# First layer's context attention: key projection of two slabs by seven products, context in two slots

## The reference

```python
def _L0_xattn_ref(query_tokens, key_tokens, key_down, query_down, query_down_bias, value_down, value_up):
    # H, T, A, C = (8, 512, 64, 128)
    def swishmax(x, axis):
        m = jnp.max(x, axis=axis, keepdims=True)
        xe = x * jnp.exp(x - m)
        return xe / (jnp.sum(jnp.abs(xe), axis=axis, keepdims=True) + 1.0)
    k = jnp.einsum('bkt,hta->bhka', key_tokens, key_down)
    q = jnp.einsum('bqt,hta->bhqa', query_tokens, query_down) + query_down_bias[None]
    logits = jnp.einsum('bhka,bhqa->bhkq', k, q)
    attn = swishmax(logits, axis=-2)
    vs = jnp.einsum('bhkq,bkt->bhqt', attn, key_tokens)
    vs = jnp.einsum('bhqc,hct->bhqt', jnp.einsum('bhqt,htc->bhqc', vs, value_down), value_up)
    return vs.sum(axis=1)
...
    x = x + _L0_xattn_ref(_layernorm(x, axis=-1), ctx_1024, L0_xattn_key_down, ...)
```

## Time and profile before

| | us |
|---|---|
| median of 3 runs | 4138.32 (4137.81 to 4142.93) |
| the profiled execution, its own time | 4137.65 |
| its span, first to last instruction | 4135.9 |
| TensorE busy | 4021.5 (97%) |
| VectorE busy | 2258.6 (55%) |
| ScalarE busy | 1402.9 (34%) |
| GpSimd busy | 428.6 (10%) |

### The profile page before, as it was taken

One profiled execution on the slowest core, in us unless ns is written; L12 is line 12 of the kernel. 1 busy time (PEld: TensorE's weight loads), 2 busy tenths in 40 slices (PEclk: granted clock), 3 DMA queues, 4 the chain that ended last, 5 costly groups with the idle time before them and its releaser, 6 DMA issues. The chain is left out here.

```text
span 4135.9 us, 69396 instructions
## 1 busy us (share of the span) xinstructions
PE 4021.5 (97%) x28288; PEld 2796.1 (68%) x28288; DVE 2258.6 (55%) x4772; ACT 1402.9 (34%) x3796; POOL 428.6 (10%) x407
## 2 busy tenths in 40 slices
PE   8999999999999999999899999999999999999897
PEld 4777777777777778677465445666666666676675
DVE  5555555555555555255544224666666666656556
ACT  3222223232323232144232002444444444443344
POOL 2020202020202020022211000000000000000222
PEclk9999999999999999999999999999999999999999
DMA  4111111121111112210303200101101101101000
GB/s 143 62 62 62 62 62 62 62 62 62 62 62 62 62 62 72 88 42 22 127 22 103 107 1 26 55 29 42 55 24 44 55 14 57 52 1 44 12 2 21
DMA packets 123703, 219.59 MB, mean 53 GB/s; under 512 B 9088, under 2 KB 47616, under 8 KB 121600
## 3 DMA queue, kind: packets, MB, share of 16 engines
q1 hardware_dynamic: 110208, 166.91, 12.2%
q0 software_dynamic: 13184, 48.24, 3.7%
HBM read 198.35 MB, written 16.78 MB: 52 GB/s over the span
## 5 line engine op out<-in xcount | busy, mean ns | idle before, releaser
L577 PE MATMUL swishmax_attended<-swishmax_weights_t,swishmax_context 128*128 128x128 f32 x4096 | 520.1, 275 | 3.4 <-DVE swishmax_values_t L505 3.4
L577 PEld LDWEIGHTS swishmax_attended<-swishmax_weights_t,swishmax_context 128*128 128x128 f32 x4096 | 487.9, 192 | 3.8 <-issue 3.8
L1504 PE MATMUL context_bank<-ahead_stream,ahead_staged 128*128 128x512 f32 x1024 | 473.0, 605 | 1.3 <-PEq L1072 1.3
L1370 ACT ACTIVATE context_exps<-context_score,context_neg_max 128x512 f32<-128x512 f32 x512 | 345.1, 686 | 379.0 <-DVE context_neg_max L1402 379.0
L591 PE MATMUL swishmax_bank<-ahead_stream,ahead_w 128*128 128x512 f32 x1024 | 463.5, 596 | 7.3 <-DMA ahead_stream<-in_context_t_dram 7.3
L435 ACT ACTIVATE swishmax_xes<-swishmax_score,swishmax_neg_max 128x512 f32<-128x512 f32 x256 | 177.2, 694 | 808.3 <-DVE swishmax_neg_max L470 808.3
L577 PE MATMUL swishmax_attended<-swishmax_weights_t,swishmax_sides 128*128 128x128 f32 x3072 | 384.8, 275 | 0.0
L1402 DVE TENSOR_REDUCE context_neg_max<-context_score 128x1 f32<-128x512 f32 x512 | 317.8, 683 | 105.3 <-PE context_score L1472 104.5
L1504 PEld LDWEIGHTS context_bank<-ahead_stream,ahead_staged 128*128 128x128 f32 x1024 | 184.2, 189 | 280.8 <-issue 273.9
L577 PEld LDWEIGHTS swishmax_attended<-swishmax_weights_t,swishmax_sides 128*128 128x128 f32 x3072 | 363.6, 192 | 0.0
L591 PEld LDWEIGHTS swishmax_bank<-ahead_stream,ahead_w 128*128 128x128 f32 x1024 | 185.7, 191 | 198.7 <-issue 196.4
(11 more groups left out here) (340 smaller groups left out, 5639.5 us busy)
## 6 DMA issues: line engine op xcount, KB each, us to landing
ahead_stream<-in_context_t_dram SPq DMA_DIRECT2D x78, 1024.0 KB, 5.4
swishmax_context<-in_context_dram POOLq DMA_DIRECT2D x32, 1024.0 KB, 5.8
swishmax_down<-_L_xattn_value_down_dram SPq DMA_DIRECT2D x64, 256.0 KB, 4.9
swishmax_up<-in_L_xattn_value_up_dram SPq DMA_DIRECT2D x32, 512.0 KB, 6.4
ahead_values<-ahead_staged SPq DMA_DIRECT2D x14, 1024.0 KB, 8.8
context_values<-ahead_values POOLq DMA_DIRECT2D x56, 256.0 KB, 3.5
experts_w<-in_L_ffn_W_dram SPq DMA_DIRECT2D x16, 512.0 KB, 8.4
whole_x<-in_x_dram SPq DMA_DIRECT2D x8, 256.0 KB, 9.3
```

What stands on the lines that cost most here:

```text
L577: last = nc.tensor.matmul(product(i)[:, m, :], side(left, c, k, m), weights_t[:, n % 2, right, k, :], start=c == 0 and k == 0 and m == 0 a ...
L1370: nc.scalar.activation(exps[:, n % EXPS, r, :], score[r][:], ACT.Exp, bias=neg_max[:, u % 2, r, c:c + 1], accum_out=total[:, u % 2, r, c:c ...
L1504: last = nc.tensor.matmul(bank_t[:], w["k"][:, k, g * P:(g + 1) * P], context_t[:, c, k, :], start=k == 0, stop=k == DC - 1)
```

## The change

Keys are computed for two slabs at once, in 16 pairs q (NQ) of units. The product of the two slabs (256 columns) with a chunk of `context_t` is split into 2x2 blocks and done by seven block products instead of eight (two matmuls of 256 columns each), in four tiles of the ring ("prod", i = 0 to 3: P1 and P6, P7 and P5, P2 and P3, P4). The sums of slab blocks are made once by VectorE (`key_sides`), the sums of context blocks for every chunk and pair by GpSimd (`combine_context_t`, four operations of 512 elements). VectorE makes the seven sums that give the keys, with ScalarE copying P1 to SBUF first; ScalarE's copy of the key tile is gone. For a chunk the tiles are spread over two steps: in an odd step i = 0 stands where the key tile stood and i = 1 behind `attend`, in an even step i = 2 and i = 3. The keys of the pair are made eight steps ahead, so the last fall in step 120.

`context_t` has two slots instead of four, since the sums take the other two; it is loaded for each pair (64 loads instead of 32), each load behind the last tile of the chunk that used the slot. The context fetches move from GpSimd's queue to SP's. `down` and `up` have one slot instead of two, and a slab's load waits for the output of the unit before. `values`: ScalarE copies one product instead of two, VectorE makes all seven sums, GpSimd none. The `unused` tile has one slot. Core of the diff:

```diff
+        context_t = [ahead.stream[:, 2 * n] for n in range(2)]
+        spare = [ahead.stream[:, 2 * n + 1].rearrange("p c k -> p (c k)") for n in range(2)]
+        context_sides = [t[:, 0:3 * D].rearrange("p (s k n) -> p s k n", k=2, n=2 * P) for t in spare]
+        first_sum, u2, u3, u4 = (t[:, 3 * D + 2 * P * n:3 * D + 2 * P * (n + 1)] for t in spare for n in range(2))
+        key_sides = s.sb("key_sides", [P, NG // 2, 3, 2, P])
...
+        def key_tiles(n):
+
+            if n < 1 or (n - 1) // (2 * NCH) + 1 >= NQ:
+                return [], []
+            q, (c, half) = (n - 1) // (2 * NCH) + 1, divmod((n - 1) % (2 * NCH), 2)
+            tiles = prod(q, c)[2 * half:2 * half + 2]
+            return tiles[:1], tiles[1:]
...
-            key, turned = [("key", u + 1, c)] * (u + 1 < NU), [("turned", u - 1, c, r) for r in range(HG)] * (1 <= u <= NU)
...
+            key, key_late = key_tiles(n)
+            turned = [("turned", u - 1, c, r) for r in range(HG)] * (1 <= u <= NU)
+            out = early_keys + [("score", u, c)] * (u < NU) + late_keys
             out += key + turned if n <= LAG else turned[:1] + key + turned[1:]
-            out += [("attend", (n - LAG) // NCH, (n - LAG) % NCH)] * (0 <= n - LAG < NU * NCH)
+            out += [("attend", (n - LAG) // NCH, (n - LAG) % NCH)] * (0 <= n - LAG < NU * NCH) + key_late
             out += [("inner", (n - LAG) // NCH - 1)] * (n - LAG >= NCH and (n - LAG) % NCH == 0)
...
+                out += [("exp", u, c, 0)] * (u < NU) + turned + [("exp", u, c, 1)] * (u < NU) + firsts(key)
...
+            out = early_keys + [("max", u, c, r) for r in range(HG)] * (u < NU) + [("weigh", u, c, r) for r in range(HG)] * (u < NU)
+            out += late_keys + key + [("turned", u - 1, c, 1)] * (1 <= u <= NU)
...
+            out += key_late + [("inner", (n - LAG) // NCH - 1)] * (n - LAG >= NCH and (n - LAG) % NCH == 0)
             out += [("output", (n - LAG) // NCH - 1)] * (n - LAG >= NCH and (n - LAG) % NCH == 1)
             out += [("values", (n - LAG) // NCH, 1)] * (n - LAG >= 0 and (n - LAG) % NCH == NCH - 1)
...
+                def load_context_t(q, c):
+                    n = q * NCH + c
+                    if n >= 2:
+
+                        last = ("prod", (n - 2) // NCH, (n - 2) % NCH, 3)
+                        sp.wait_ge(full_d, ring.count(last))
...
+                load(sp, w_key[:, :, 0:2 * P], a["key_down"][:, 0:2 * P], w_loaded["first_key"])
                 load_context_t(0, 0)
                 sp.dma_start(x_sb[:, 0, :], x_dram[0]).then_inc(first_x_loaded, 16)
                 sp.dma_start(ident[:], ident_dram).then_inc(ready, 16)
+                load_context_t(0, 1)
                 load(sp, w_query[:], a["query_down"], w_loaded["query"])
                 sp.dma_start(q_bias[:], a["query_bias"]).then_inc(w_loaded["query"], 16)
-                load_context_t(0, 1)
-                load(sp, w_key[:, :, P:], a["key_down"][:, P:], w_loaded["key"])
+                load(sp, w_key[:, :, 2 * P:], a["key_down"][:, 2 * P:], w_loaded["key"])
+                load_context_t(0, 2)
                 for b in range(1, B):
...
+                load_context(0, 0)
+                load_context_t(0, 3)
+                load_context(0, 1)
+                load_context_t(1, 0)
+                load_context(0, 2)
+                load_context_t(1, 1)
+                load_context(0, 3)
+                load_slab(0)
+                for n in range(STEPS):
+
+                    m = n // 2 + 1 + NCH
+                    if n % 2 == 0 and m >= NCH + 2 and m < NQ * NCH:
+                        load_context_t(m // NCH, m % NCH)
+                    b, c = divmod(n - 1, NG * NCH)
+                    if n > 1 and 1 <= b < B and c < NCH:
+                        load_context(b, c)
+                    u, c = divmod(n - 6, NCH)
+                    if u >= 1 and c == 0 and u < NU:
                         load_slab(u)
-                    if u == NU - 2 and c < 2:
-                        sp.wait_ge(full_a, ring.count(("key", NU - 1, c)))
-                        ahead.load(sp, c)
-                sp.wait_ge(full_a, ring.count(("key", NU - 1, NCH - 1)))
+                last = ("prod", NQ - 1, NCH - 1, 3)
...
+                def combine_context_t(q, c):
+                    n = q * NCH + c
+                    pool.wait_ge(ctx_t_landed[n % 2], 16 * (n // 2 + 1))
+                    raw = context_t[n % 2]
+                    b11, b12, b21, b22 = raw[:, 0:2, 0:2 * P], raw[:, 0:2, 2 * P:], raw[:, 2:4, 0:2 * P], raw[:, 2:4, 2 * P:]
+                    t1, t2, t4 = (context_sides[n % 2][:, k] for k in range(3))
+                    link(nc.gpsimd.tensor_tensor(t1, b12, b11, ALU.subtract))
+                    link(nc.gpsimd.tensor_tensor(t2, b22, t1, ALU.subtract))
+                    link(nc.gpsimd.tensor_tensor(b12, b22, b12, ALU.subtract))
+                    link(nc.gpsimd.tensor_tensor(t4, t2, b21, ALU.subtract))
+                    pool.sem_inc(ctx_t_sided, 1)
+
+                for c in range(NCH):
+                    combine_context_t(0, c)
+                    if c:
+                        combine_sides(0, c - 1)
+                combine_context_t(1, 0)
+                combine_sides(0, NCH - 1)
+                for n in range(NU * NCH):
+
+                    m = (n + 1) // 2 + NCH
+                    if n % 2 and m < NQ * NCH:
+                        combine_context_t(m // NCH, m % NCH)
+                    b, c = divmod(n - 2, NG * NCH)
+                    if n > 2 and 1 <= b and c < NCH:
+                        combine_sides(b, c)
 
...
+                    elif what == "prod":
+                        c = t[2]
+                        act.wait_ge(full_d, ring.count(t))
+                        if u or c:
+
+                            act.wait_ge(out_d, ring.count(("prod", u - (c == 0), (c - 1) % NCH, 2)))
+                        nc.scalar.copy(first_sum, ring.bank(t)[:, 0:2 * P]).then_inc(first_copied, 1)
...
+                        v2, v3, v4 = (partial[:, i] for i in range(3))
+                        link(nc.vector.tensor_tensor(v2, first_product[:], product(P6), ALU.add))
+                        nc.vector.tensor_tensor(values_t[:, 0:2, 0, :], first_product[:], product(P2), ALU.add)
+                        nc.vector.tensor_tensor(v3, v2, product(P7), ALU.add)
+                        link(nc.vector.tensor_tensor(v4, v2, product(P5), ALU.add))
+                        nc.vector.tensor_tensor(values_t[:, 0:2, 1, :], v4, product(P3), ALU.add)
+                        nc.vector.tensor_tensor(values_t[:, 2:4, 0, :], v3, product(P4), ALU.subtract)
+                        nc.vector.tensor_tensor(values_t[:, 2:4, 1, :], v3, product(P5), ALU.add).then_inc(values_out_d, 1)
...
+                        if i == 0:
+                            dve.wait_ge(first_copied, u * NCH + c + 1)
+                            last = nc.vector.tensor_tensor(u2, first_sum, halves_of[1], ALU.add)
+                        elif i == 1:
+                            dve.wait_ge(out_d, ring.count(("prod", u, c, 0)))
+                            link(nc.vector.tensor_tensor(u3, u2, halves_of[0], ALU.add))
+                            nc.vector.tensor_tensor(u4, u2, halves_of[1], ALU.add)
+                            last = nc.vector.tensor_tensor(even[:, 2 * P:], u3, halves_of[1], ALU.add)
+                        elif i == 2:
+                            dve.wait_ge(out_d, ring.count(("prod", u, c, 1)))
+                            nc.vector.tensor_tensor(odd[:, 0:2 * P], first_sum, halves_of[0], ALU.add)
+                            last = nc.vector.tensor_tensor(odd[:, 2 * P:], u4, halves_of[1], ALU.add)
+                        else:
+                            last = nc.vector.tensor_tensor(even[:, 0:2 * P], u3, halves_of[0], ALU.subtract)
+                        last.then_inc(out_d, 1)
...
+                        pe.wait_ge(key_sided, u % 2 + 1)
+                        pe.wait_ge(ctx_t_sided, n + 1)
+                        for i, which in enumerate(KEY_TILES[t[3]]):
+                            left, right = PRODUCTS[which]
+                            for k in range(2):
+                                last = nc.tensor.matmul(bank_t[:, 2 * i * P:2 * (i + 1) * P], key_side(left, u % 2, k), context_side(right, n % 2, k),
```

More of the change, by code:

```diff
@@ L318, in dve_step @@
             b, g = divmod(u, NG)
-            out = [("max", u, c, r) for r in range(HG)] * (u < NU) + [("weigh", u, c, r) for r in range(HG)] * (u < NU)
-            out += [("turned", u - 1, c, 1)] * (1 <= u <= NU)
+            early_keys, late_keys = first_keys(n)
+            key, key_late = key_tiles(n)
+            out = early_keys + [("max", u, c, r) for r in range(HG)] * (u < NU) + [("weigh", u, c, r) for r in range(HG)] * (u < NU)
+            out += late_keys + key + [("turned", u - 1, c, 1)] * (1 <= u <= NU)
             if c < NCH - 1:
@@ L366, in _ @@
-                for n in range(NU * NCH):
```

(40 more changed lines are left out.)

152 lines of the change are left out of this document (80 added, 72 removed).

## The result

| | before | after |
|---|---|---|
| median, us | 4138.8 | 4205.2 (4204.1 to 4211.4, 4 runs) |
| ratio after to before | | 1.0162, 95% interval 1.0144 to 1.0179 |
| profiled execution and its span | 4137.65, 4135.9 | 4204.08, 4202.3 |
| start of the score of step 5 | 64.75 | 106.04 |
| four steps of the steady state | 50.63 | 50.67 |

A forecast was written before the change was run, and what follows sets the result against it. TensorE, busy 1099.83 of 1100 us in the attention over the context, was taken as the bound. From 4137.65 us: -55 +48 +1.5 +25 +28.5 = +48, so 4185.7, rounded 4186; range 4142 to 4235.

The forecast's parts named there:

- the boundaries: Seven batch boundaries, where GpSimd's context sums queue behind its new sums and delay VectorE: 25 us lost (0 to 45).
- Part 1: Seven products on TensorE: 28 records of 256 columns take 6.00 us for 6.86, saving 55 us (38) over 64 chunks.
- the rival of bare weight loads: Added weight loads on TensorE not overlapped: 11.3 us for 6.86, 284 in all, time over 4400; chance 0.02.
- Part 2: What the key tile no longer hides: 28 waits of 1.70 us before second transposes, 48 us; steps without keys 1.5.
- Z: Time zero in the step n mod 4 = 1: end of the unit's last `attend`; bank empty forecast at Z+5.84.
- tile B: Key tile behind `attend`, 1.72 us in odd steps, 0.86 in even ones; VectorE must empty it before `values`.
- the walk: The forecast's step-by-step timing of the engines, from which the waits, boundary losses and start loss were taken.
- Part 3: GpSimd and VectorE: SBUF-only sums wait for GpSimd's instructions; free in regular steps, 3.6 us at each of seven boundaries.
- regular kind 3 steps: Steps n mod 4 = 3 away from batch boundaries: `scale` ends before tile B is full, free with 0.2 us to spare.
- the rival that put a price on each of them: GpSimd's lock delays `scale` in every n mod 4 = 3 step: 21 units x 1.3 = 27, so 4213; chance 0.17.
- the last one of the working: At a boundary: `scale` late, tile B empty at 16.7, second transposes at 18.7 instead of 15.1, 3.6 us each.
- Part 4: The start: GpSimd's sums and the load order put step 4's score at 91.8, now 57.70; 28.5 us lost (18 to 38).

The follow-up runs named there:

- attend first: Changed kernel with `attend` put ahead of the second head's transposes in steps n mod 4 = 1 that still have key tiles: 4206.5 us, ratio 1.0163.
- values first: Changed kernel with VectorE doing the sums of `values` ahead of, not behind, the sum of the key tile behind `attend`: 4194.1 us, ratio 1.0128.
- sides later: Changed kernel with GpSimd's sums of the context's second chunk at batch boundaries held until `scale` is done: 4170.6 us, ratio 1.0075.
- all three: Changed kernel with attend first, sides later, and a start with x loads and third-chunk context_t sums moved ahead: 4155.3 us, ratio 1.0043.
- all sides later: The all three kernel with the sums of the context's fourth chunk also held until `scale` is done: 4122.5 us, ratio 0.996.

## Why the prediction came out as it did

Direction and mechanism held, and the size was short by 18 us, mainly in two terms: the boundaries (8 us) and the start (7 us). In the order of steps, with the start of each score in the two traces:

| | forecast | measured |
|---|---|---|
| shift at the score of step 4, then 5 | +34.1 | +39.7, +41.3 |
| steady state, to step 120 | 0 | +1.6 |
| seven boundaries | +25 | +33.4 |
| end, to step 124 (forecast: what the sum leaves) | -11 | -9.9 |
| in all | +48 | +66.4 |

**Part 1 was right.** A record of 256 columns is half one of 512: 0.216 us, so 28 of them take 6.05 us (6.00 taken, 6.26 the other bound), and 64 times the difference to 6.86 is 52 us. The doubled loads, 197 ns each, are hidden behind records 0.216 us apart, as the rows of before had it; the rival of bare weight loads has fallen.

**Part 2 was right in place, count and size.** There are 28 waits, and attend first, which takes them away, shortens each unit by 1.69 us (50.67 to 48.98), where 1.70 was forecast. VectorE's maximum starts at Z+3.97 (3.89 forecast), and the bank is free at Z+5.91 (5.84). The records before it end by their distances at Z+4.24 (4.14 forecast): the change from tile B to the score costs 0.10 us that the walk left out. The 1.50 in the list of waits is less because it counts from a modelled end. The other side of the balance came out too: without the wait a unit takes 1.65 us less than the old 50.63, where 1.72 was forecast. With it the units are equal, 50.67 to 50.63. The second run that bears on the chain is values first, where the wait in the list shrinks to 1.04 us.

**Part 3: mechanism right, size too small.** The regular kind 3 steps are free (the cut of the sums there changed nothing), and the rival that put a price on each of them has fallen. The boundaries cost 4.8 us each, not 3.6: the step behind a boundary lasts 17.08, 14.12, 15.69, 15.84, 15.79, 15.66 and 15.73 us instead of 10.93. The step that failed is the last one of the working, which turned the delay on VectorE into time one to one, at full clock. TensorE's two waits are nearly the same at all seven (1.95 to 2.18 and 0.79 us); the clock is not:

```profile
511.87:525.99 14.12, 11.26 (x81) 9.47 (x81) 10.39 (x21) 3.46 (x8) 7.70 (x7) 1.00 0.19 70
726.22:729.63 3.41, 3.27 (x8) 2.64 (x9) 2.66 (x5) 2.54 (x6) 3.17 (x4) 0.50 0.00 0
```

In the second of the seven steps (the first row is the whole of it) the clock stays at 1.00, and 3.19 us are lost. In five it is at 0.50 for 3.4 us (the second row is one of them), and 4.73 to 4.91 are lost. In the first it is at 0.50 for 6.8 us, and 6.15 are lost. In the values first run the same two waits stand at the seven boundaries, and the losses again go with the clock: 3.08, 3.17 and 3.26 us where it stays, 4.61 to 4.90 where it is low for 3.4 us, 6.03 where for 6.8. So the meeting alone costs some 3.2 us each, a little less than the 3.6 of the walk, and the other 11 of the 33.4 us are the clock, which the walk put at nothing. The Trainium skill's sentence on an exclusive lock between the two engines ("SBUF — State Buffer", section "SBUF: two separate sides") fits the rows: VectorE's small SBUF sums and `scale` are held up beside GpSimd (1.11 us for 0.17, 1.96 for 0.88), and in the run in which the same sums come behind `scale` they cost nothing.

**Part 4: mechanism right, size too small by 7 us.** TensorE stands idle from 33.2 to 45.9 us where 34 to 44 was forecast, and step 4's score is at 97.35, not 91.8. The order of events was as walked, and two things in it were too small. The first is the clock. The walk names one low-clock price, 1.8 us at the beginning, and its 7.8 us for the third chunk's products (44.1 to 51.9) hold a second one. But TensorE stands idle four times for GpSimd, and after three of them the first four key records take 2.04 or 2.05 us instead of 1.03, and it is low again after the wait for VectorE that the walk had:

```profile
12.93 2.04 PE L693 MATMUL swishmax_bank<-ahead_stream,ahead_w 128*128 128x256 f32 x4 [12.93 <-POOLq L477]
45.88 2.05 PE L693 MATMUL swishmax_bank<-ahead_stream,ahead_w 128*128 128x256 f32 x4 [12.65 <-POOLq L477]
73.73 2.05 PE L693 MATMUL swishmax_bank<-ahead_stream,ahead_w 128*128 128x256 f32 x4 [7.86 <-POOLq L477]
90.20 2.58 PE L662 MATMUL swishmax_score<-swishmax_keys_t,swishmax_queries_t 64*128 64x512 f32 x4 [6.98 <-DVE swishmax_xes L546]
92.71 2.08 PE L693 MATMUL swishmax_bank<-ahead_stream,ahead_w 128*128 128x256 f32 x4
```

From step 3's score to step 4's it takes 7.15 us where the walk had 4.5; the score and the first key group behind it, 1.13 and 1.03 us at full clock, take 2.58 and 2.08. The second is the queue: GpSimd starts on the first context chunk at 34.9 us, and not at 33, and each later event slips with it. The third chunk's sums end at 45.7 (44.1 forecast), the next pair's first sums at 73.5 (70.8), and step 3's score starts at 90.2 (87.3). These two make the 5.6 us at step 4. The last 1.6, to step 5, the walk did not look at.

## What to carry to other kernels

Work moved to an idle engine is not priced by that engine's share: look up which operations of its neighbour lie in the same microseconds, and put the moved work where the neighbour reads PSUM, or where nobody waits for the neighbour. Here the same GpSimd sums, held back by a few us, gave 35 us at one place per batch (sides later) and 33 at another (all three to all sides later). With the orders on TensorE and in the start they turned a change that lost 1.6% into one that gained 0.4%. Before a long tile is split, walk every chain that it hid from its start to the bank that it frees; and when an edit removes a wait and the time stays, compare the list of waits, for the new one has a name.

## What was not expected of the hardware

TensorE's granted clock fell to 0.50 at six of the seven boundaries (waits of some 2.06 and 0.79 us, 0.63 us of work between them), and after a single wait of 3.34 us in the attend first run, but not after the single waits of 1.50 us in 28 kind 1 steps; the clock of the stretch from 400 to 1500 us, with both in it, is 0.99. The same pair of waits so cost 3.2, 4.8 or 6.1 us, by how long the clock stayed low. What decides between them is not shown: the waits are alike (2.07 and 0.79 us at the boundary that kept the clock, 2.06 and 0.79 at the next). In the run with all sides later neither kind is left and the stretch is at 1.00.
